# Ordering the indirect DMAs of one POOL step: four gathers then four scatters, instead of in turn

## The reference, cut to what matters

```python
h = jnp.maximum(_layernorm(x, axis=-1), 0.0)
s, v = h[:, :64] @ W_nl0, einsum('nmi,mk->nki', h_vectors, W_nl1)
w = relu(edge_feature @ W_fc1) @ W_fc2              # 224 weights per edge
xs, xv = s[dst], v[dst]                             # the gather
tp = concatenate([w0*xs, w3*(xv . sh1), w1*xs*sh1, w2*xv, w4*cross(xv, sh1)])
agg = segment_sum(tp, src, num_segments=N) / 32.0   # the scatter
out_s = agg_s @ W_out_s + s_skip                    # likewise the vectors
x = x + concatenate([silu(out_s[:, :64]), sigmoid(gate) * out_v])
```

## Time and profile before

| | |
|---|---|
| time, median of 3 runs | 1494.89 us (1494.34 to 1687.11) |
| span of the profiled execution, first to last instruction | 1490.1 us |
| instructions | 23,307 |
| POOL busy | 1134.9 us (76% of the span) |
| PE busy | 1184.7 us (80%) |
| DVE busy | 891.4 us (60%) |
| ACT busy | 451.2 us (30%) |
| 16 DMA engines, POOL's queue | 36.0% |
| mean granted TensorE clock | 0.749 of full speed |

### The profile page before, as it was taken

One profiled execution on the slowest core, in us unless ns is written; L12 is line 12 of the kernel. 1 busy time (PEld: TensorE's weight loads), 2 busy tenths in 40 slices (PEclk: granted clock), 3 DMA queues, 4 the chain that ended last, 5 costly groups with the idle time before them and its releaser, 6 DMA issues.

```text
span 1490.1 us, 23307 instructions
## 1 busy us (share of the span) xinstructions
PE 1184.7 (80%) x5766; PEld 975.6 (65%) x5766; DVE 891.4 (60%) x3688; ACT 451.2 (30%) x868; POOL 1134.9 (76%) x853
## 2 busy tenths in 40 slices
PE   8889788787887879788787878889787887878800
PEld 5668667676766667677676767767676776767700
DVE  6429556665656666555566656556665656666519
ACT  4234323233332323323232332323232232332300
POOL 1417888888888888888888888888888888888864
PEclk7559967778777877868777786877787687786855
DMA  5444545545454544545445454544545454554574
GB/s 225 153 154 95 96 79 91 84 77 98 75 93 83 89 86 77 98 75 93 82 87 88 75 100 75 92 83 86 90 76 99 75 91 84 84 90 69 68 195 158
DMA packets 118198, 144.09 MB, mean 97 GB/s; under 512 B 30880, under 2 KB 91552, under 8 KB 118176
## 3 DMA queue, kind: packets, MB, share of 16 engines
q0 software_dynamic: 79872, 75.03, 36.0%
q1 hardware_dynamic: 36576, 61.34, 13.1%
q10 hardware_dynamic: 1728, 7.47, 1.2%
HBM read 88.56 MB, written 55.21 MB: 96 GB/s over the span
## 4 chain that ended last, share of the span: by engine, by line
issue 29%; POOL 27%; DMA 24%; PE 11%; DVE 7%; POOLq 1%; DVEq 1%; ACT 0%; ACTq 0%
DMA sums<-to_add,add_idx 19%; POOL rows L302 16%; POOL sums L320 11%; DMA rows<-node_table,to_idx 4%; PE o_ps L460 2%; PE w_ps L427 2%; DVE products_space L757 1%; DVE products_space L728 1%; PE t_ps L442 1%; PE d_ps L475 1%; PE d_ps L398 1%; DVE products_space L755 1%; PE d_ps L396 1%; PE o_ps L396 1%; PE o_ps L398 1%
## 5 line engine op out<-in xcount | busy, mean ns | idle before, releaser
L320 POOL DMA_INDIRECT sums<-to_add,add_idx x416 | 678.1, 1630 | 126.7 <-issue 118.8
L302 POOL DMA_INDIRECT rows<-node_table,to_idx x416 | 424.6, 1021 | 193.9 <-issue 119.3
L728 DVE TENSOR_TENSOR products_space<-rows,rhat 128x256 f32<-128x256 f32 (+2 forms) x520 | 170.3, 394 | 506.2 <-DMA rows<-node_table,to_idx 506.2
L460 PEld LDWEIGHTS o_ps<-w,pT 128*128 128x128 f32 (+1 forms) x2496 | 414.2, 252 | 40.1 <-issue 32.8
L460 PE MATMUL o_ps<-w,pT 128*128 128x96 f32 (+1 forms) x2496 | 431.3, 340 | 0.0
L442 PE MATMUL t_ps<-w,products_space 128*128 128x128 f32 (+1 forms) x1248 | 237.7, 324 | 213.6 <-DVE products_space L757 208.0
L442 PEld LDWEIGHTS t_ps<-w,products_space 128*128 128x128 f32 (+1 forms) x1248 | 182.2, 171 | 233.4 <-issue 221.9
L427 PE MATMUL w_ps<-w,hid 64*128 64x224 f32 x832 | 283.6, 475 | 0.8 <-ACT hid L568 0.7
L576 ACT ACTIVATE pT<-t_ps 128x512 f32<-128x512 f32 (+1 forms) x312 | 185.2, 594 | 262.0 <-PE t_ps L442 239.0
L585 ACT ACTIVATE msg<-o_ps 128x448 f32<-128x448 f32 x208 | 113.0, 543 | 409.9 <-PE o_ps L460 364.4
L427 PEld LDWEIGHTS w_ps<-w,hid 64*128 64x128 f32 x832 | 180.7, 240 | 59.3 <-issue 49.2
(11 more groups left out here) (115 smaller groups left out, 557.7 us busy)
## 6 DMA issues: line engine op xcount, KB each, us to landing
from_row<-nodes_row SPq DMA_DIRECT2D x52, 512.0 KB
ef<-edge_t SPq DMA_DIRECT2D x52, 256.0 KB
rows<-node_table,to_idx POOLq DMA_INDIRECT x416
sums<-to_add,add_idx POOLq DMA_INDIRECT x416
sums<-zeros ACTq DMA_DIRECT2D x8, 672.0 KB
sums<-zeros SPq DMA_DIRECT2D x4, 672.0 KB
x_sb<-x SPq DMA_DIRECT2D x5, 400.0 KB, 6.6
node_table<-node_rows SPq DMA_DIRECT2D x5, 400.0 KB, 2.4
```

The lines of the kernel that those rows point to most:

```text
L302: pool.indirect_dma_start(rows[:, u, j, SC:CR], None, table, bass.IndirectOffsetOnAxis(ap=to_idx[:, par, h * J + j:h * J + j + 1], axis=0) ...
L320: pool.indirect_dma_start(sums[j], bass.IndirectOffsetOnAxis(ap=add_idx[:, u, j:j + 1], axis=0), to_add[:, u, j, :], None, compute_op=ALU.add,
L460: ins = nc.tensor.matmul(o_ps[m][:, base + oc:base + oc + n], pT[c][u % 2][:, cols], w[0:ROWS[c], wc:wc + n], start=(q == 0 and c == 0), s ...
L728: ins = nc.vector.tensor_tensor(vecs(crs[:, dst, :, i0 * V:(i0 + n) * V], n), vecs(rows[:, u, :, VE + v0 * V:VE + (v0 + n) * V], n), unit( ...
```

## The change

Within each of POOL's steps the loop over the four tiles is split in two. Before, each pass issued gather j of group g + 3 and then scatter j of group g - 4. Now the four gathers of group g + 3 come first, and the four scatters of group g - 4 follow. The waits move with the calls to which they belong. The number of instructions, DMAs and bytes is the same.

```diff
             def steps(i):
                 for u in range(UNROLL):
                     g = UNROLL * i + u
                     for j in range(J):
                         gather(g + LEAD, (u + LEAD) % UNROLL, j, i + (u + LEAD) // UNROLL)
+                    for j in range(J):
                         scatter(g - LAG, (u - LAG) % UNROLL, j)
```

## The result

The change makes the kernel faster: 1449.23 us (1445.01 to 1468.5, 4 runs) against 1494.62 us, a ratio of 0.970 (95% interval 0.966 to 0.973). In two later comparisons, on two chips, the changed kernel came to 0.977 (0.968 to 0.987) and 0.978 (0.970 to 0.986). Both are clear of no change, but their intervals reach across 0.980, so they do not settle whether the gain is over 2%. The ratios take the faster of two states of the chip alone, and the medians all runs. The forecast was 1466.3 us, a ratio of 0.981; within its range (1446 to 1490 us) the result lies 3 us from the lower end.

What follows compares the result with a forecast made beforehand. The prediction took POOL's own time on eight indirect DMAs a step as the bound. From a span of 1490.1 us it took 21.8 (order) and 6.8 (stretching), giving 1461.5, plus 4.8 to the median: 1466.3 us, range 1446 to 1490.

Steps and rivals of the forecast that it cites:

- The bound: In the loop, POOL's own time on eight indirect DMAs a step, not their transfers, sets the 13.06 us step.
- Part (a), the order: POOL's DMAs: only those following the other kind cost 38 or 37 ns extra; saving 225 ns a step, 21.8 us.
- the sign that I had named: POOL's medians in L302 and L320 become 953 and 1553 ns, with the first of each kind at 991 and 1590.
- Part (a), the stretching: DVE's two-input operations lengthen single POOL DMAs; 0.29 us a step falls to 0.22, gaining 6.8 us.
- The layout of starts: Counted from DVE's start, POOL's scatters start at about -1.95, -0.05, 1.80, 3.65 us, gathers at 5.5, 6.8, 8.1, 9.3.
- Part (b), the waits: Waits of gathers, scatters, DVE's L819 and SP's reload in the loop: shifted slack stays covered, cost 0.
- Part (c): Kernel's ends: nothing changes ahead of step 4, 13 us of slack at the end only grows, PE still fits.
- that stretching vanishes: Rival 1, POOL against DVE: contention all but vanishes, gain 50 us, time 1445 us; chance 0.20.
- The one on the slow side: Rival 2: POOL's starts lock onto DVE's two-input operations, +47 us, time 1542 us; chance 0.06.
- PE did not take over: Rival 3: PE's clock falls below 0.71, PE needs as long as a step, time 1485 to 1495 us; chance 0.08.
- rival 4: 953 and 1553 ns belong to the kernel's quiet ends, not same-kind neighbours; only contention moves, about 1488 us; chance 0.11.
- The 4.8 us that I added: Whole time: the median stands 4.8 us above the span, taking the forecast from 1461.5 to 1466.3 us.

Runs made afterwards that it cites:

- three pairs of profiles: Kernel before and changed kernel, each profiled three times, the last two without edits: ratios before 1.007 and 0.997, changed 0.970, 0.977 and 0.978.
- Pairs: Kernel before with two gathers, two scatters, two gathers, two scatters in each POOL step: ratio 1.006 (1.001 to 1.011), step 13.04 us.
- The twin: Same DMA order, but L728, L738, L770, L781 cut to one element per partition; in changed order median 1449.13 us, no ratio, step 12.67 us.
- second profile: Changed kernel run and profiled again without any edit: ratio 0.977 (0.968 to 0.987) against the kernel before, 1445.25 us.
- third profile: Changed kernel run and profiled once more without any edit: ratio 0.978 (0.970 to 0.986) against the kernel before.
- the twin of pairs: Two gathers, two scatters, twice a step, with DVE's four two-input operations cut to one element per partition: ratio 0.998 (0.989 to 1.006), step 12.98 us.
- the twin in turn: Kernel before, order unchanged, with DVE's four two-input operations cut to one element per partition: ratio 0.987 (0.984 to 0.990), step 12.81 us.
- the scatters first: Kernel before with the four scatters of each POOL step ahead of its four gathers: ratio 0.983 (0.970 to 0.996), step 12.75 us.

## Why the prediction was right or wrong

**The bound: right.** POOL was continuously at work before and is after, 0.3 us at most between two DMAs. Only its own time per DMA counted. The first stage aside, the forecast of 28.6 us (21.8 + 6.8) met 27.0, 29.1 and 27.0 us in the three pairs of profiles, and the step of 12.76 us met 12.74 to 12.78.

**Part (a), the order: the mechanism right, the size wrong.** I charged 38 and 37 ns to the first of each kind and nothing to the others, as measured where one kind stands alone, and took the price of a change of kind to be the same whatever went before. The runs show otherwise, and so does the sign that I had named: in the profile after, 200:1340 us, the medians are 964 and 1580 ns and not 953 and 1553, and the first of a kind is not at 991 and 1590. After a run of two or four of the other kind, the first costs 1.02 and 1.62 us and the second still 0.97 and 1.57 to 1.59; only from the third on is it 0.95 and 1.55. So a change of kind is paid on the two DMAs behind it. From these, a step of the changed kernel holds 1.02 + 0.97 + 2 x 0.95 + 1.62 + 1.57 + 2 x 1.55 = 10.18 us of DMA work where it held 4 x (0.99 + 1.59) = 10.32 before. The term was 0.225 us a step and measured 0.14: 97 x 0.14 = 13.6 us, and not 21.8. Pairs show the same law from the other side: 10.38 us, more than in turn.

**Part (a), the stretching: the cause right, the size wrong the other way.** Two-input operations of DVE do stretch POOL's DMAs. The twin with these operations cut shows it: the 0.24 us by which its step in turn is shorter (13.05 to 12.81). The rule of the Trainium skill ("SBUF — State Buffer", Who interferes with whom), that a VectorE instruction with two SBUF inputs contends with a GpSimd instruction that reads SBUF, holds here. The inference in the same list (that tensor_tensor does not stall descriptor generation) I took to be refuted by the gather at 708.80, and that went too far: only the start of the instruction was held up, and the scatter of 713.89, with L771 and L739 running inside it, was not. No run here contradicts it. I put the stretching after the change at 0.22 us a step. Measured it is 4 x (983 + 1601) ns less the 10.18 us of bare work, which gives 0.16 us, and with the second profile's 982 and 1593 ns 0.12 us; before it was 0.29. So this term was 0.07 and measured 0.13 to 0.17, or 13 to 16 us. The layout of starts held to within 0.35 us: in the step shown the second scatter began 0.30 us behind DVE's start and not 0.05 ahead of it, and took 1.57 us all the same, since the one of L729's five multiplications that was running ends 0.12 us later, at 712.14, and the DMA does not wait for those behind it. The third scatter (713.89, 1.55 us) is clear although L758 runs above it. L758 takes one input from PSUM. The first trace of the kernel before bears this out: in 200:1370 us, 83 DMAs had such an operation (L754, L755 or L757) and none with two SBUF inputs running 0.12 us into them, and not one was over 0.99 or 1.59 us by more than 0.02. The two wrong sizes cancel, which is luck: 13.6 + 15 against 21.8 + 6.8.

**Part (b), the waits: right for POOL, incomplete for ACT.** DVE's start (7 us forecast, 6.7 measured) and L819 behaved as laid out: L820 waited for scatters once, 0.7 us, in the profile after and 10.5 us in five waits in the second. In the twin, whose DVE has less to do, the same wait grew to 157.4 us in 83, and POOL's gaps stayed at 0.3 us. The first scatter of a step, for which (b) has 5.2 us and the layout of (a) 5.05, came at 5.11. What I left out is ACT's `collect`, which waits for the scatters of the group four before. The sums are ready sooner while those scatters land no sooner, and so ACT now waits for them: 54.7 us in 22 waits of up to 3.2 us, and PE 29.8 us behind ACT (in the second and third profile 37.7 and 24.5 us, and PE 0.7 in each). It costs nothing, since POOL sees no gap from it, but slack that I had booked as free was partly used.

**Part (c) and the rivals.** The ends cost nothing. Of the rivals, that stretching vanishes was half true. The one on the slow side was not seen: no run had more stretching a step than the 0.29 us of before, though in the twin of pairs it rose to 0.17 us, where the twin in turn had 4 x (996 + 1598) ns less 10.32, which is 0.06. PE did not take over, and rival 4 fell with the first look at the durations.

**The whole time** came out 17 us below the forecast on record. Of these, 12.2 are in the span (1461.5 forecast, 1449.3 measured). The first stage is what the forecast didn't have: I read 51.9 us to the first gather as fixed, and it wanders from 38 to 52 us between executions of either kernel (56 with the scatters first). In the profiles it made 13.7 us of the 40.8. The other 4.9 us are the step from span to median. The 4.8 us that I added do not "cover what lies around the span": the profiled run after took 1451.14 us with a span of 1449.3, so 1.8 us lie around it, and the rest was the difference between two executions. Whether the first stage made all of what is left in the timed runs isn't shown, since of each set of runs only one has a profile; the two later comparisons came to 0.977 and 0.978, near the forecast's 0.981. It is luck, too, that 1449.2 us fell inside the range and to the faster side of 2%, for which the prediction had a chance of 0.39: the loop alone gives 27 to 29 us, just under 2%.

## What to carry to other kernels

When an engine shows 76% busy and gaps that are all alike and have no releaser, it is full; count what it spends on each instruction, and by what stands before it in the queue. On POOL, put indirect DMAs of one kind together in runs of four; runs of two gave nothing, and longer ones were not timed. And when two effects of an edit are worked out from a stage where neither stands alone, run the twin that silences one: a right sum can hide two wrong terms.

## What the runs showed of the hardware

- POOL's time on an indirect DMA depends on the two before it: a gather of 128 rows of 640 bytes takes 0.99 us in turn with scatters, and 1.02, 0.97, 0.95, 0.95 in a run; an adding scatter of 128 rows of 768 bytes takes 1.59 in turn, and 1.62, 1.57, 1.55, 1.55. The first of a run is the same after two and after four of the other kind (1.02, 1.62).
- A DVE operation that reads two tensors in SBUF, and runs about 0.12 us into the DMA instruction of POOL, holds that instruction until the operation ends (up to 0.4 us); one that starts later in it did nothing (L771 and L739 inside the scatter of 713.89). Seen for L728, L738, L770, L781 and L796; an operation with one input in PSUM (L758) did nothing.
- The first stage of 38 to 56 us follows TensorE's granted clock, for one and the same program. In the five profiles with a clock of 1.00 from 20 to 30 us and 64 multiplications there, the first gather came at 38.2 to 38.3 us. In the other seven PE did 36 or 37 in these ten microseconds, and it came at 48.9 to 56.1; six of them have the clock at 0.50, and the seventh (scatters first) has no record of it there.
